# Residual plus attention added in place ahead of the batches, and two seams around the attention inputs reordered

## What is computed

```
x = layernorm(x + retention(x))              # 16 heads of 16
x = layernorm(x + ternary_ffn(x))            # 256 -> 1024 -> 256, gelu and a layernorm between
a = per_token_attention(x)                   # q, k, v projections; then, for each token by itself, heads against heads
x = layernorm(x + (gelu(a @ W1.T) @ W2.T + a))
x = layernorm(x + mixture_of_experts(x))     # 8 experts, top 2
```

## Time and profile before

| | us |
|---|---|
| median of 3 runs | 1154.15 |
| lowest, highest | 1150.55, 1155.3 |
| the profiled execution | 1152.17 |
| its span, first to last instruction | 1150.5 |

### The profile page before, as it was taken

One profiled execution on the slowest core, in us unless ns is written; L12 is line 12 of the kernel. 1 busy time (PEld: TensorE's weight loads), 2 busy tenths in 40 slices (PEclk: granted clock), 3 DMA queues, 4 the chain that ended last, 5 costly groups with the idle time before them and its releaser, 6 DMA issues. The chain is left out here.

```text
span 1150.5 us, 22668 instructions
## 1 busy us (share of the span) xinstructions
PE 889.0 (77%) x8214; PEld 701.1 (61%) x8214; DVE 715.7 (62%) x1553; ACT 484.8 (42%) x1140; POOL 219.2 (19%) x308
## 2 busy tenths in 40 slices
PE   3687888878849999993989598971787864999960
PEld 2576666666636777762434387850465653999960
DVE  5256556665563677775889536788256577655628
ACT  1143443334417777761964234553333320444520
POOL 0111222212220213212000000000122104365333
PEclk9799999999978999995999799995888865999995
DMA  6100000000000000000477444410522121364528
GB/s 202 33 20 11 19 18 9 18 9 18 0 0 1 1 1 1 2 1 0 110 152 177 92 107 114 101 36 0 189 73 70 41 73 35 96 168 126 175 40 275
DMA packets 74614, 75.26 MB, mean 65 GB/s; under 512 B 26032, under 2 KB 68144, under 8 KB 73392
## 3 DMA queue, kind: packets, MB, share of 16 engines
q1 hardware_dynamic: 70576, 69.08, 20.7%
q0 software_dynamic: 3968, 5.25, 2.8%
HBM read 46.51 MB, written 27.79 MB: 65 GB/s over the span
## 5 line engine op out<-in xcount | busy, mean ns | idle before, releaser
L591 DVE TENSOR_TENSOR r_prob<-r_pS,const 128x512 f32<-128x512 f32 x128 | 79.5, 683 | 41.9 <-PE r_pS L461 41.9
L1073 DVE SCALAR_TENSOR_TENSOR f_gl<-f_g,lnw,f_gh 128x512 fp32r<-128x512 f32 x64 | 47.3, 747 | 40.4 <-ACT f_gh L1011 38.1
L1729 POOL TENSOR_TENSOR m_s<-x_res,att_res 128x1024 f32<-128x1024 f32 (+1 forms) x8 | 18.8, 2345 | 269.6 <-SPq L111 269.6
L1274 PE MATMUL q_pE<-q_xT,att_res 128*128 128x512 f32 x128 | 61.1, 634 | 6.7 <-ACT q_xT L1220 6.7
L952 PE MATMUL f_pY<-wpjT,f_gh 128*128 128x256 f32 x256 | 65.2, 289 | 0.0
L953 PE MATMUL f_pY<-wpjT,f_gl 128*128 128x256 f32 x256 | 62.7, 279 | 0.0
L952 PEld LDWEIGHTS f_pY<-wpjT,f_gh 128*128 128x128 f32 x256 | 48.1, 188 | 15.5 <-issue 13.4
L1005 ACT ACTIVATE f_g<-f_pH 128x512 f32<-128x512 f32 x64 | 38.0, 594 | 38.5 <-PE f_pH L941 37.7
L582 DVE COPY r_kT<-r_pKK 128x256 f32<-128x256 f32 x32 | 13.6, 424 | 65.3 <-PE r_pKK L446 65.2
L941 PE MATMUL f_pH<-f_xh,wfcT 128*128 128x512 f32 x128 | 52.7, 412 | 1.4 <-DVE f_xl L1067 1.4
L2278 DVE SCALAR_TENSOR_TENSOR e_hl<-e_pH,e_hh 128x320 fp32r<-128x320 f32 x64 | 27.6, 483 | 39.4 <-ACT e_hh L2241 39.3
(11 more groups left out here) (297 smaller groups left out, 2560.8 us busy)
## 6 DMA issues: line engine op xcount, KB each, us to landing
kv_dram<-att_res SPq DMA_DIRECT2D x16, 512.0 KB, 4.1
t_ring<-kv_dram SPq DMA_DIRECT2D x128, 64.0 KB, 2.3
wi<-L_ffn_wi SPq DMA_DIRECT2D x8, 1024.0 KB, 5.6
wo<-L_ffn_wo SPq DMA_DIRECT2D x8, 1024.0 KB, 8.6
r_xin<-L_attn_x SPq DMA_DIRECT2D x32, 128.0 KB, 2.0
q_dram<-att_res SPq DMA_DIRECT2D x8, 512.0 KB, 3.1
t_q<-q_dram SPq DMA_DIRECT2D x64, 64.0 KB, 3.2
x_dram<-x_res SPq DMA_DIRECT2D x8, 512.0 KB, 3.0
```

The lines of the kernel that those rows point to most:

```text
L591: dve.tensor_tensor(prob[t % 2][:, r, :, :], pS[r][:, :, :], dec[:, r, :, :], ALU.mult)\
L1073: dve.scalar_tensor_tensor(out=gl[c % 4][:, :], in0=g[c][:, :], scalar=net.lnw[:, c:c + 1], in1=gh[c % 4][:, :], op0=ALU.mult, op1=ALU.sub ...
L1274: mm = pe.matmul(out[:, :], net.wqkvT[:, k, n * P:(n + 1) * P], xT[p][:, k, :], start=(k == 0), stop=(k == KD - 1))
```

## The change

The last batch of the FFN leaves the shared loop: its `moments` come first, then `norm(6)`, `base`, `shifts`, and a new `last_rows` that runs each of the four kinds of operation for all four tiles before it waits. The phase of the attention inputs no longer waits for its stores; SP waits for them where the attention's loads need them, and DVE before it first writes `att_res`. The very last of the six items of the last batch (half of v) is copied by ACT and no longer by DVE. In the attention the `pA` banks are cleared first and PE starts after these, and waits for `pO` before the first mix. And in the MLP POOL adds all eight batches at the phase's beginning, in place into `x_res`, and DVE reads `x_res` where it read `s`; `s` is gone.

```diff
+        def last_rows(b):
+            dve.wait_ge(down_made.sem, down_made.after(NH * (b + 1)))
+            for t in range(TPB):
+                ins = dve.scalar_tensor_tensor(out=xb[:, t, :], in0=net.u1[:, :], scalar=shift[:, t:t + 1], in1=xb[:, t, :],
+                                               op0=ALU.mult, op1=ALU.add)
+            ins.then_inc(steps.sem, 1)
+            dve.wait_ge(steps.sem, steps.done(1))
...
+        moments(BATCH - 1)
+        norm(BATCH - 2)
+        base(BATCH - 1)
+        shifts(BATCH - 1)
+        last_rows(BATCH - 1)
         norm(BATCH - 1)
```

```diff
     def _(sp):
         for b in range(BATCH):
             for n in range(3):
-                sp.wait_ge(item_ready.sem, item_ready.after(ITEMS * b + KD * (n + 1)))
+                last = b == BATCH - 1 and n == 2
+                sp.wait_ge(item_ready.sem, item_ready.after(ITEMS * b + KD * (n + 1) - last))
+                if last:
+                    sp.wait_ge(last_value.sem, last_value.after(1))
...
-        for n in range(3):
-            sp.wait_ge(stored[n].sem, stored[n].after(16 * BATCH))
...
+        act.wait_ge(v_made.sem, v_made.after(2 * BATCH))
+        act.wait_ge(stored[2].sem, stored[2].after(16 * (BATCH - 1)))
+        for half in two:
+            dst = res[2][0:ROWS4, :, 2 + half]
+            ins = nc.scalar.activation(dst, pV[1][half * ROWS4:(half + 1) * ROWS4, :], ACT.Copy)
+        ins.then_inc(last_value.sem, 1)
...
         for m in range(1, CHUNKS):
+            if m >= 2 and m % 2 == 0:
+                for n in range(3):
+                    sp.wait_ge(net.stored[n].sem, net.stored[n].after(16 * (m + 2)))
...
+            if n == 2:
+                pe.wait_ge(cleared.sem, cleared.after(2))
...
+            if u == 0 and r == 0:
+                for n in range(3):
+                    dve.wait_ge(net.stored[n].sem, net.stored[n].after(16 * BATCH))
...
-        for i in two:
-            dve.memset(pA[i][:, :, :], 0.0)
-            ins = dve.memset(pO[i][:, :, :], 0.0)
-        ins.then_inc(cleared.sem, 1)
+        for bank in (pA, pO):
+            for i in two:
+                ins = dve.memset(bank[i][:, :, :], 0.0)
+            ins.then_inc(cleared.sem, 1)
```

```diff
         def base(b):
-            pool.wait_ge(y_taken.sem, y_taken.after(2 * b))
-            pool.sem_inc(net.passed_pool, 1)
-            pool.tensor_tensor(s[:, :, :], net.x_res[:, bass.ds(b * TPB, TPB), :], net.att_res[:, bass.ds(b * TPB, TPB), :], ALU.add)\
-                .then_inc(s_ready.sem, 1)
+            tiles = slice(b * TPB, (b + 1) * TPB)
+            pool.tensor_tensor(net.x_res[:, tiles, :], net.x_res[:, tiles, :], net.att_res[:, tiles, :], ALU.add).then_inc(s_ready.sem, 1)
 
         def body(b, before, behind):
             pool.wait_ge(mv_ready.sem, mv_ready.after(b + 1))
             rstd_of(pool, steps, yrs[:, :], ymv[:, :, 1], LN_EPS, net).then_inc(yrs_ready.sem, 1)
-            if behind:
-                base(b + 1)
-
-        base(0)
+
+        for b in range(BATCH):
+            base(b)
         all_batches(pool, body, steps, 1)
...
-                dve.tensor_tensor(y[:, 2 * h:2 * h + 2, :], pY[h][:, :, :], s[:, 2 * h:2 * h + 2, :], ALU.add).then_inc(y_taken.sem, 1)
+                dve.tensor_tensor(y[:, 2 * h:2 * h + 2, :], pY[h][:, :, :], net.x_res[:, bass.ds(b * TPB + 2 * h, 2), :], ALU.add)\
+                    .then_inc(y_taken.sem, 1)
```

More of the change, by code:

```diff
@@ L1115, in rows @@
                 ins.then_inc(rows_ready.sem, 1)
+        def last_rows(b):
[5 more added lines that the diff above has]
+            dve.wait_ge(steps.sem, steps.done(1))
+            for t in range(TPB):
+                ins = dve.scalar_tensor_tensor(out=y[:, t, :], in0=pY[b % 2][t // 2][:, t % 2, :], scalar=rs[:, t:t + 1], in1=xb[:, t, :],
+                                               op0=ALU.mult, op1=ALU.add)
+            ins.then_inc(steps.sem, 1)
+            dve.wait_ge(steps.sem, steps.done(1))
+            for t in range(TPB):
+                ins = dve.bn_stats(yst[:, t, :], y[:, t, :])
+            ins.then_inc(steps.sem, 1)
+            dve.wait_ge(steps.sem, steps.done(1))
+            dve.wait_ge(q_rs_ready.sem, q_rs_ready.after(b))
+            for t in range(TPB):
+                ins = dve.bn_aggr(ymv[:, t, :], yst[:, t, :])
+            ins.then_inc(rows_ready.sem, 1)
         def norm(b):
@@ L1125, in _ @@
             low(0, k)
-        for b in range(BATCH + 1):
+        for b in range(BATCH):
             for c in range(NH):
-                if b < BATCH:
-                    low_part(b, c)
+                low_part(b, c)
                 if b and c == 1:
@@ L1160, in attention_inputs @@
     net.q_in = [Signal(net, net.projections, f"q_in{i}") for i in two]
+    net.stored = [Signal(net, net.projections, f"kept{n}", 16) for n in range(3)]
     net.signals = own
@@ L1181, in attention_inputs @@
     item_ready = ph.sig("item_ready", 6)
-    stored = [ph.sig(f"stored{n}", 16) for n in range(3)]
+    stored, last_value = net.stored, ph.sig("last_value")
     step, nothing_ready = ph.sig("step"), ph.sig("nothing_ready")
@@ L1299, in body @@
                 norm(b + 1, 1 - p)
-            for n in range(ITEMS):
+            for n in range(ITEMS - (not behind)):
                 if n % KD == 0:
```

1 line of the change is left out of this document (removed).

## The result

| | before | after |
|---|---|---|
| median, us | 1153.38 (1150.55 to 1155.3, 4 runs) | 1122.01 (1121.48 to 1124.15, 4 runs) |
| the profiled execution, us | 1152.17 | 1121.61 |
| its span, us | 1150.5 | 1119.9 |

The ratio is 0.9731, with a 95% interval of 0.9712 to 0.975: 31 us faster. 1125 was forecast, with 1117 to 1135 as the range. The spans differ by 30.6 us, and they are what can be taken apart.

What follows compares the result with a forecast made beforehand. It took waits and the DVE–POOL–PE chain, with `xn` held by POOL's add, as the bound; 2.1 + 6.9 + 13.9 + 6 - 0.8 - 0.2 = 27.9 us gave 1124.3, stated as 1125, range 1117 to 1135.

Steps and rivals of the forecast that it cites:

- The tail, 2.1: End of the FFN: moments taken first save 1.0 us and `last_rows` without waits 1.1, together 2.1 us.
- The seam, 6.9: Between attention inputs and attention: fewer DVE copies, no wait for stores landing (5.8 us), two memsets fewer before PE (1.1).
- `xn`, 13.9: MLP loop: L1930 no longer held by POOL's add in seven of eight groups, saving 13.9 us.
- rival (d): MLP `xn`: L1930 is long for another reason than POOL's add, giving 1144 us; chance 0.04.
- The clock, 6: MLP turns: PE's clock falls less often once its wait closes; 6 us taken, between nothing and some 9.
- Rival (a): MLP turns: the clock keeps falling on the logits, giving 1130 us; chance 0.20.
- The price of the casts, 0.8: MLP start: POOL's adds may hold DVE's casts and delay PE; 0.8 us taken, bounds 0 to 3.3.
- Rival (b): MLP start: POOL's first adds hold both DVE casts and POOL is late for root 0, giving 1128 us; chance 0.13.
- POOL's run of adds: MLP start: eight adds of 2.35 us, 18.8 in all, end about when the first root is wanted; up to 0.2 us.
- rival (c): MLP start: POOL's adds take longer than 18.8 us and delay root 0; 1161 us at 7 us each; chance 0.01.
- DVE's y operations beside the adds, nothing: MLP phase: DVE's y operations read PSUM and SBUF, so running beside POOL's adds costs them nothing.
- The 0.2 us for an address: MLP loop: DVE now works out an address for `x_res`, costing 0.2 us in all.

Runs made afterwards that it cites:

- e8: The changed kernel with SP again waiting for its stores at the end of the attention inputs: 1126.76 us, ratio 0.9766.
- e9: The changed kernel with the last item's second pair of copies on DVE again instead of ACT: 1123.41 us, ratio 0.976.
- e4_adds_late: The kernel before, with POOL's add for the next batch waiting until DVE has written this batch's normed rows: 1132.99 us, ratio 0.9825.
- e11: The changed kernel with four unread DVE additions ahead of the `xn` operations of batches 0 to 6, POOL idle: 1145.86 us, ratio 0.9949.
- e5_casts_first: The changed kernel with POOL's eight adds not starting before DVE's second cast is done: 1118.63 us, ratio 0.971.
- e7_adds_twice: The changed kernel with each of POOL's eight adds preceded by a second one into an unread tile: 1134.56 us, ratio 0.9846.
- e3_adds: The kernel before with only POOL's eight adds moved ahead and made in place: 1129.47 us, ratio 0.9808.
- e6_two_us: The changed kernel with one unread DVE addition ahead of the `xn` operations of batches 0 to 6: 1130.63 us, ratio 0.9801.
- e12_filled: The changed kernel with four unread DVE additions ahead of `xn` and four unread matmuls in PE's wait, batches 0 to 6: 1139.68 us, ratio 0.9901.
- e13_best: The changed kernel with DVE's casts before POOL's adds, plus six unread matmuls ahead of batch 5's attention transposes: 1123.57 us, ratio 0.9756.

## Why the prediction was right, point by point

**The forecast of 1124.3 us for an execution like the profiled one** came out as 1121.6, with terms of 27.9 us where 30.5 were found. The 1125 is not quite its sum: with the whole 2 us by which the median lay above the profiled execution it would be 1126.3. After the change the two differ by 0.4 us.

- *The tail, 2.1:* 2.0 in after's trace. From `outer(6)` to `shifts` it gave 0.8 us (1.0 in the sum), and `last_rows` 1.2 (1.1).
- *The seam, 6.9:* 6.7. ACT's two copies took 2.16 us and were over by 641.6, under the cover of DVE's own, which ended at 643.4. The landing was worth 3.5 (e8), ACT's copy 2.1 (e9), the parted memsets 1.1.
- *`xn`, 13.9:* L1970 at 408 ns, 414 at most, in all eight groups. e4_adds_late shows that it was the coincidence with POOL's add, which rules out rival (d).
- *The clock, 6, with bounds of 0 and 9:* this term was mis-sized. From one batch's `xn` to the next, the loop is 24.7 us shorter in all; without the 13.9 that leaves 10.8. Putting the wait back cost 11.4 of clock (e11), and PE's busy time fell by 11.1. The step that failed is the choice of two thirds of the bound, and the bound itself was too low. It took half the slow time of a turn as what can come back, 1.4 to 2.9 us; half of the 3.6 and 6.3 us that it read from its rows is 1.8 and 3.2. The five turns whose wait closes gave 1.2 to 2.9 us each beyond their `xn`, 9.9 together, where some 9 were the most (the last of them went from 14.3 to 9.6 us), and the two at the choice of experts, which the bound left out, 0.9. So nearly all of the slow time that hung on these waits came back. Rival (a), that the logits alone let the clock fall, is refuted by four turns with logits at 1.00.
- *The price of the casts, 0.8, with bounds of 0 and 3.3:* mis-sized as well; it was 3.3, as PE started 4.8 us behind the first cast for 1.5. Rival (b) was right in its mechanism, and e5_casts_first gives the 3.3 us back (3.4 by the medians). The 0.8 lay below even the 1.1 us of one held cast. Both were held: the first started 0.01 us behind POOL's first add. (b)'s second half, a late first root, did not come: PE began late itself, and POOL then stood idle for 3.9 us.
- *POOL's run of adds:* 18.46 us, where 18.8 was taken. e7_adds_twice shows that rival (c)'s mechanism is real, and that in after the adds could have been 3.9 us longer at no cost.
- *DVE's y operations beside the adds, nothing:* right, they took 0.69 us beside POOL's adds in e7_adds_twice as elsewhere. The sum drew this from four L591 with a POOL operation inside, which was a multiplication of 0.73 us and no add. The 0.2 us for an address can not be told apart in the rows.
- *Not in the sum:* the attention inputs and the attention were 1.8 us shorter. No run ties that to an edit, and the same attention took 149.1 to 152.5 us over these kernels, at granted clocks of 0.85 to 0.88. I count it as scatter; its cause was not tested.

The two mis-sized terms, +4.8 and -2.5, cancelled in part, so it is partly luck that the forecast came within 3 us. The range held by its own reasons: it had taken in (a) and (b) with the casts' full price, and at its low end all the clock that I allowed.

The Trainium skill, "SBUF — State Buffer", section "SBUF: two separate sides", says that of a GpSimd operation and a DVE operation of the kinds named in the prediction, whichever starts first has the shared ports for the whole instruction. In after POOL's first add starts at 794.94, DVE's cast at 794.95, and the cast ends just behind the add: the trace agrees. It leaves open who is next when both engines want the ports. Here POOL's second add was, and the second cast lasted to its end; between 1.1 us for one held cast and 3.3 for both, that is the whole difference.

## What to carry to other kernels

Where a short DVE operation has a minimum of 400 ns and a maximum of 2434, look at what POOL starts just before it: moving POOL's adds 3 us back (e4_adds_late, 19.9 us) or ahead of the batches (e3_adds, 23.4) was worth more here than both seams together. Then look at what the moved work holds in its new place: both of these held something else. When a wait of PE is priced, add what its clock does behind it: by the traces 0.5 us more of delay in each of seven turns cost 1.0 us a turn (e6_two_us without its slow start), and 2 us cost 3.6 (e11_four_adds). And when POOL's work is moved to a phase's start, look at what DVE has there that others wait for, and let that go first.

## What the runs showed of the hardware that was not expected

- The clock can fall behind short waits. With waits of 0.18 to 0.29 us behind the eight-column logits it stood at 1.00 in four turns in a row; in e6_two_us it fell behind waits of 0.78 and 0.77 us (down took 4.35 and 5.01 us in these turns, for 3.62) and did not behind one of 0.67. With the wait filled by matmuls (e12_filled) it did not fall. The length of the wait alone doesn't decide: behind the same first wait of 2.18 us down took 3.62 us in after and e3_adds, but 3.95 in e13_best and 4.17 in e4_adds_late.
- Work that POOL does beside DVE is free or costs its whole length, depending on DVE's operation: an fp32 to bf16 cast 2.37 us for 0.23, a subtract and multiply with two per-row scalars 2.43 for 0.40, a subtraction of two SBUF inputs 2.11 for 0.29 (e4_adds_late), but an addition with one input in PSUM 0.69 for 0.69, and four bn_stats 1.40 for 1.39.
- POOL's addition of 128x1024 took 1.89 us with the same tile as both inputs, and 2.34 with two.
